# A transformer block with window attention: FC1 and the query/key projection regrouped into 128 + 64 channels

## The chip, the cores and the metric

The kernel runs on one core of a Trainium2 chip. The metric is the time of one execution on the device, in microseconds. TensorE (PE in the profile) multiplies, with the loads of its stationary operand shown apart (PEld); VectorE (DVE), ScalarE (ACT) and GpSimd (POOL) work on elements; SyncE (SP) issues every transfer of this kernel.

## What is computed

Inputs are 32 images of 96 channels and 56 x 56 pixels, in float32. The block is a Swin block with windows of 7 x 7 pixels (49 tokens), shifted by 3 pixels, and 12 heads of 8 channels:

```python
f = roll(layernorm(x over channels) * g1 + b1, (-3, -3))        # windows of 49 tokens
q, k, v = split(win @ w_qkv + b_qkv)                            # 96 -> 3 x 96
attn = softmax(q @ k.T * 8**-0.5 + mask); out = (attn @ v) @ w_proj + b_proj
f = x + unroll(out)
m = layernorm(f over channels) * g2 + b2
result = f + gelu(m @ w_fc1 + b_fc1) @ w_fc2 + b_fc2            # 96 -> 192 -> 96
```

## The kernel before

A **band** is one row of 8 windows, 7 x 56 pixels or 392 tokens (`TOK`); there are 8 bands in an image and 256 in all. The engines run the same software pipeline, written out by hand: at step t each engine works on several bands, each at another stage (`LOAD` t+9, `TURN` t+6, `BACK` t+5, `QK` t+4, `KEYS` t+3, scores t+2, probabilities t, and so on). Steps alternate between an odd and an even kind with another order. Two steps are one round of the pattern, and there are 128 such pairs. Engines are ordered by semaphores alone, and each engine runs its instructions in the written order.

The stages that matter here:

- `turn` transposes a band to tokens (L472), `back` transposes the normalised tokens back to channels (L487). `back_high` and `back_low` split the result in two float16 parts, `xfh` and `xfl`, whose row 96 of ones carries the bias.
- `queries_keys` (every step) and `expand` (twice in an odd step, FC1 of two bands) multiply by a weight of 192 output channels. They do it in two halves of 96 channels, each by `three` (L379): three products over all 392 tokens (high x high, high x low, low x high) into one PSUM bank of 96 partitions. So each use is 6 matmuls, 96 columns of weights by 392 tokens.
- In an odd step both uses of `expand` stand between `turn` and `max_transpose` (L511); then come `out_transposes` (L522), `back` (L487), `queries_keys` and `project` (L532). `back` waits for `gelu_done` of both FC1 results, since ScalarE has to empty the banks. In an even step `queries_keys` stands between `max_transpose` and `project`, and `contract` (FC2 of two bands, L559, float32) follows.
- ScalarE's `gelu` (L660) reads 96 x 784 of PSUM, `queries_keys_high` (L638) reads as many and writes the high parts to `nat`; VectorE's `queries_keys_low` (L772) writes the low parts.
- `values` (L395), `scores` (L414), `shifted` (L430) and `weighted` (L446) use 49 columns of weights, alternately for PSUM partitions 0 to 48 and 64 to 112.
- SP stores `nat` to a DRAM page per band with two transfers (`save_parts`, L286 and L289), and loads it again, reordered: `key_blocks` into `qst` and `kbd` (5 transfers, L258 and L260), `stacks` into `kst` and `qbd` (5 transfers). Before `key_blocks` SP waits until the high parts have landed in the page (`high_out`). `scores` waits for `key_in`, the five landings of `key_blocks`.
- FC2's bias is a row of `w2` against a row of ones in `hid`.
- VectorE's `result` adds `f` to FC2's output, two or more steps after `turn` has read that `f`.

Of the kernel before, what the change touches and what calls it, by code (L numbers as in the profile page):

```python
# [55 lines left out]
GAIN = 64.0  # L56
# [36 lines left out]
def build(nc, x, g1, b1, wqkv, bqkv, wproj, bproj, g2, b2, wfc1, bfc1, wfc2, bfc2,  # L93
# [7 lines left out]
    with ctx:  # L101
        def sb(name, shape, dt=F32):
            return ctx.enter_context(nc.sbuf_tensor(name, shape, dt))
# [12 lines left out]
        wp, w2 = sb("wp", [FULL, C]), sb("w2", [FULL, 2, C])  # L116
        vec = sb("vec", [C, 5])
        G1, B1, BP, G2, B2 = range(5)
# [7 lines left out]
        nat = sb("nat", [C, 4, 4, TOK], F16)  # L126
# [12 lines left out]
        hid = sb("hid", [FULL, 2, 2, TOK])  # L139
# [6 lines left out]
        stack_pages = nc.dram_tensor("stack_pages", [4, 2 * (side + 3 * TOK)], F16, kind="Internal").ap()  # L146
        q_stack = [stack_pages[n, 0:side].rearrange("(c m t) -> c m t", m=3, t=TOK) for n in range(4)]
        k_stack = [stack_pages[n, TOK + side:TOK + 2 * side].rearrange("(c m t) -> c m t", m=3, t=TOK) for n in range(4)]
        both_parts = [stack_pages[n, TOK:TOK + 2 * side].rearrange("(s c m t) -> c s m t", s=2, m=3, t=TOK)[:, :, 0:2, :] for n in range(4)]
        high_parts = [stack_pages[n].rearrange("(s r) -> s r", s=2)[:, 0:side].rearrange("s (c m t) -> c s m t", m=3, t=TOK)[:, :, 0, :] for n in range(4)]  # L150
# [12 lines left out]
        STACK_IN, KEY_IN = 5 * 16, 5 * 16  # L163
        X_IN = [16] * 7 + [2 * 16]
# [10 lines left out]
        ot_made, o_in, proj_made, f_made = sem("ot_made"), sem("o_in"), sem("proj_made"), sem("f_made")  # L175
        fc1_made, gelu_done, fc2_made, y_made = sem("fc1_made"), sem("gelu_done"), sem("fc2_made"), sem("y_made")
# [39 lines left out]

        @block.sync
        def _(sp):
# [10 lines left out]
            const(wp[0:C, :], wproj)  # L229
            for m in range(2):  # L230
                const(w2[0:C, m, :], wfc2[m * C:(m + 1) * C, :])
            const(w2[C:C + 1, 0, :], bfc2.rearrange("(a c) -> a c", a=1))
            const(brow[C:C + 1, :], bqkv.rearrange("(a c) -> a c", a=1))
            const(brow1[C:C + 1, :], bfc1.rearrange("(a c) -> a c", a=1))
            for n, v in ((G1, g1), (B1, b1), (BP, bproj), (G2, g2), (B2, b2)):
                column(n, v)
# [15 lines left out]
            def key_blocks(b):  # L252
# [3 lines left out]
                sp.wait_ge(high_out[b.c % 4], b.used(4, 16))  # L256
# [6 lines left out]
            def stacks(b):  # L263
# [3 lines left out]
                sp.wait_ge(nat_out[n], b.used(4, 16))  # L267
# [12 lines left out]
            def save_parts(b):  # L280
# [33 lines left out]
        def _(pool):  # L314
# [21 lines left out]

            def normalise(b):
# [19 lines left out]
            def step(t):  # L357
                if turns(t.step(TURN)):
                    normalise(t.step(TURN))
                if has(t.step(ORDER)):  # L360
                    order_x(t.step(ORDER))

# [3 lines left out]
        def _(pe):  # L366
# [123 lines left out]
            def queries_keys(t):  # L490
# [9 lines left out]
                for m in range(2):  # L500
                    last = three(psum[0:C, at + m, 0:TOK], wh[:, m * C:(m + 1) * C], wl[:, m * C:(m + 1) * C], b, 0)
                last.then_inc(qk_made, 1)
# [31 lines left out]
            def expand(t, n):  # L534
# [9 lines left out]
                for m in range(2):  # L544
# [322 lines left out]
```

## Time and profile before

| | |
|---|---|
| median of 3 runs | 3063.34 us (3062.35 to 3064.25) |
| the profiled execution, whole | 3062.91 us |
| its span, first to last instruction | 3061.1 us |
| mean granted clock of TensorE | 0.992 of full speed |
| TensorE matmul busy | 2862.6 us (94%) |
| VectorE, ScalarE, GpSimd busy | 2424.3, 2076.6, 1454.5 us (79%, 68%, 48%) |
| mean busy share of the DMA queue of SP | 43.7% of 16 engines |

Busy times are unions over the engine's instructions. A matmul's recorded length is from its start to the end of its results, and matmuls overlap, so the distance from start to start is what one costs in a row of them. In the trace, "128x392" is the moving operand and "128\*96" the stationary one; a float32 matmul that is no transpose appears as two passes. "[0.47 <-issue]" behind a row is the idle time before it and what ended it.

### The profile page before, as it was taken

What the parts mean: (1) busy time and instruction counts of PE and PEld (TensorE: products, weight loads), DVE (VectorE), ACT (ScalarE), POOL (GpSimd) and SP (SyncE); (2) the same over time, 40 slices, a digit from 0 to 9 for tenths busy, and PEclk for the clock granted to TensorE, in tenths of its full rate; (3) what the DMA queues carried; (4) which work ended last, traced back from release to release, by engine and by line L of the source; (5) the groups of instructions that cost most, each with busy time, mean ns of one, the idle gap of its engine ahead of it and who ended that gap; (6) DMA issues with size and microseconds to landing.
All of it is one profiled execution on the core that took longest, in us unless ns stands there. A gap on an engine that the chain in (4) does not pass through costs nothing.

```text
span 3061.1 us, 137479 instructions
## 1 busy us (share of the span) xinstructions
PE 2862.6 (94%) x53060; PEld 2299.2 (75%) x53060; DVE 2424.3 (79%) x7208; ACT 2076.6 (68%) x3208; POOL 1454.5 (48%) x1832
## 2 busy tenths in 40 slices
PE   1799999999999999999999999999999999999997
PEld 0677777777777777777777777777777777777775
DVE  5778888788887888788787888878888788888885
ACT  0467767667776767767766767767767667777674
POOL 2554454454444444444444454444454454445444
PEclk9899999999999999999999999999999999999999
DMA  1444444444444444444444444444444444444441
GB/s 29 108 119 123 124 125 119 119 126 122 126 127 113 123 123 122 126 121 120 124 126 114 125 124 120 124 123 120 123 125 118 120 126 121 126 127 119 125 113 42
DMA packets 414727, 359.37 MB, mean 117 GB/s; under 512 B 63455, under 2 KB 413985, under 8 KB 414012
## 3 DMA queue, kind: packets, MB, share of 16 engines
q1 hardware_dynamic: 414028, 350.01, 43.7%
q8 instruction: 444, 7.27, 1.1%
q14 instruction: 255, 2.09, 0.2%
HBM read 193.25 MB, written 154.14 MB: 113 GB/s over the span
## 4 chain that ended last, share of the span: by engine, by line
PE 87%; issue 5%; ACT 5%; DVE 2%; POOL 1%; SPq 0%; DMA 0%; POOLq 0%; DVEq 0%; ACTq 0%
PE psum L446 18%; PE psum L379 16%; PE psum L559 11%; PE psum L430 10%; PE psum L414 8%; PE psum L472 7%; PE psum L487 6%; PE psum L532 5%; ACT probs L618 4%; PE psum L522 3%; PE psum L395 2%; PE psum L511 1%; DVE st L754 1%; POOL rs L349 0%; DVE xfl L765 0%
## 5 line engine op out<-in xcount | busy, mean ns | idle before, releaser
L618 ACT ACTIVATE probs<-psum 113x784 f32<-113x784 f32 x768 | 633.2, 824 | 652.0 <-PE psum L430 648.9
L730 DVE TENSOR_REDUCE nmax<-psum 113x16 f32<-113x784 f32 x768 | 745.3, 970 | 153.9 <-PE psum L414 153.3
L342 POOL TENSOR_SCALAR ve<-mv 98x8 f32<-98x8 f32 x264 | 64.5, 244 | 1482.4 <-DVE mv L759 1476.5
L446 PE MATMUL psum<-vbd,probs 128*49 128x18 f32 x24576 | 644.2, 198 | 9.8 <-issue 9.0
L446 PEld LDWEIGHTS psum<-vbd,probs 128*49 128x49 f32 x24576 | 634.4, 126 | 14.1 <-issue 13.3
L349 POOL TENSOR_TENSOR rs<-ve,half 98x8 f32<-98x8 f32 x264 | 440.0, 1667 | 0.0
L430 PE MATMUL psum<-qbd,kst 128*49 128x196 f16 x6144 | 405.1, 251 | 36.3 <-DVE xfl L765 23.2
L754 DVE BATCH_NORM_STATS2 st<-tok 98x6 f32<-98x96 f32 x2112 | 363.6, 245 | 84.3 <-ACT tok L625 70.8
L354 POOL TENSOR_TENSOR xn<-xn,rs 98x768 f32<-98x768 f32 x264 | 388.4, 1471 | 72.7 <-POOL rs L349 72.7
L414 PE MATMUL psum<-kbd,qst 128*49 128x196 f16 x6144 | 401.4, 250 | 7.6 <-issue 4.2
L765 DVE TENSOR_TENSOR xfl<-psum,xfh 96x784 f16<-96x784 f32 x264 | 256.0, 970 | 176.0 <-ACT xfh L630 174.2
L345 POOL TENSOR_TENSOR xn<-tok,mv 98x768 f32<-98x768 f32 x264 | 389.5, 1475 | 0.2 <-POOL ve L342 0.2
L559 PE MATMUL psum<-hid,w 128*96 128x392 f32 x1024 | 359.3, 494 | 0.9 <-ACT hid L660 0.9
L430 PEld LDWEIGHTS psum<-qbd,kst 128*49 128x49 f16 x6144 | 238.8, 104 | 142.1 <-issue 103.0
L414 PEld LDWEIGHTS psum<-kbd,qst 128*49 128x49 f16 x6144 | 265.0, 104 | 85.3 <-issue 80.6
L559 PEld LDWEIGHTS psum<-hid,w 128*96 128x96 f32 x1024 | 167.4, 164 | 171.9 <-issue 170.6
L638 ACT ACTIVATE nat<-psum 96x784 f16<-96x784 f32 x256 | 209.9, 820 | 121.0 <-PE psum L379 121.0
L487 PE MATMUL psum<-ident,xn 98*96 98x98 f32 x2112 | 227.8, 252 | 64.9 <-issue 57.1
L630 ACT ACTIVATE xfh<-psum 96x784 f16<-96x784 f32 x264 | 215.3, 815 | 78.3 <-PE psum L487 78.2
L612 ACT ACTIVATE vbd<-psum 49x384 f32<-49x384 f32 x512 | 261.1, 510 | 7.6 <-PE psum L395 1.1
L487 PEld LDWEIGHTS psum<-ident,xn 98*96 98x96 f32 x2112 | 189.3, 128 | 91.0 <-issue 81.1
L772 DVE SCALAR_TENSOR_TENSOR nat<-psum,nat 96x784 f16<-96x784 f32 x256 | 245.7, 960 | 0.0
(83 smaller groups left out, 5270.1 us busy)
## 6 DMA issues: line engine op xcount, KB each, us to landing
stack_pages<-nat SPq DMA_DIRECT2D x256, 294.0 KB, 3.0
kst<-stack_pages SPq DMA_DIRECT2D x256, 220.5 KB
qbd<-stack_pages SPq DMA_DIRECT2D x1024, 55.1 KB
stack_pages<-nat SPq DMA_DIRECT2D x256, 147.0 KB, 2.0
xr<-in_x_dram SPq DMA_DIRECT2D x224, 147.0 KB, 3.4
out_dram<-yr SPq DMA_DIRECT2D x224, 147.0 KB, 2.2
qst<-stack_pages SPq DMA_DIRECT2D x256, 73.5 KB
kbd<-stack_pages SPq DMA_DIRECT2D x1024, 18.4 KB
```

The source lines that it names most:

```text
L345: nc.gpsimd.tensor_tensor(xn[:, n, :, :], tok[:, n, :, :, :].rearrange("t k p c -> t (k p) c"), mv[:, n, :, 0:1].to_broadcast(wide_by_toke ...
L349: nc.gpsimd.tensor_tensor(rs[:, n, :], ve[:, n, :], half[0:PT, :], ALU.pow).then_inc(root_done, 1)
L354: nc.gpsimd.tensor_tensor(xn[:, n, :, :], xn[:, n, :, :], rs[:, n, :].rearrange("t (g a) -> t g a", a=1).to_broadcast(wide_by_token), ALU. ...
L379: last = nc.tensor.matmul(dst, weights, tokens[:, b.c % 4, kind, :], start=n == 0, stop=n == 2)
L414: last = nc.tensor.matmul(psum[W1 * w:W1 * w + L, A + p // 2, p % 2 * CH:(p % 2 + 1) * CH], qst[:, masked_slot(b), u, toks], kbd[:, b.c % ...
L430: last = nc.tensor.matmul(psum[W1 * w:W1 * w + L, B + p // 2, p % 2 * CH:(p % 2 + 1) * CH], kst[:, masked_slot(b), u, toks], qbd[:, b.c % ...
L446: last = nc.tensor.matmul(dst[:, :, h, :], probs[:, b.c % 2, h // 4, p, h % 4 * L:(h % 4 + 1) * L], vbd[:, b.c % 4, p * NH + h, :, :], sta ...
L487: last = nc.tensor.transpose(psum[0:C, B + kind, p * PT:(p + 1) * PT], xn[:, b.c % 2, kind * PAIRS + p, :], ident[0:PT, 0:PT])
L559: last = nc.tensor.matmul(psum[0:C, D + n, 0:TOK], w2[:, m, :], hid[:, b.c % 2, m, :], start=m == 0, stop=m == 1)
L618: nc.scalar.activation(probs[0:PR, b.c % 2, u, :, :].rearrange("j (g q) k -> j g (q k)", g=2), psum[0:PR, B:B + 2, 0:2 * CH], ACT.Exp).the ...
L730: nc.vector.tensor_reduce(dst, psum[0:PR, A:A + 2, 0:2 * CH].rearrange("i g (q h j) -> i g q h j", q=2, j=L), axis=AX.X, op=ALU.max, negat ...
L754: last = nc.vector.bn_stats(st[:, n, g, :], tok[:, n, g // PAIRS, g % PAIRS, :])
```

## The change

FC1 and the queries and keys now make the first 128 of their 192 output channels for all 392 tokens (3 matmuls with 128 columns of weights), and the other 64 channels for each half of the tokens apart (`PART`, 196): 6 matmuls with 64 columns, alternately for PSUM partitions 0 to 63 and 64 to 127. The result stands as 128 x 3 x 196 in PSUM where it was 96 x 2 x 392. ScalarE's GELU and high parts and VectorE's low parts read that in one instruction each. FC2 has `w2` in three parts and makes each half of the tokens with two matmuls. Row 97 of `hid` and `w2` is no longer there for the bias, so GpSimd adds FC2's bias to `f` in place, in a new stage `add_bias`, and `result` waits for it. `save_parts` needs 4 transfers for the high parts and 3 for both parts, 7 where there were 2.

```diff
+PART = TOK // 2
+REST = HID - 128
+BIAS = -4
-        wp, w2 = sb("wp", [FULL, C]), sb("w2", [FULL, 2, C])
+        wp, w2 = sb("wp", [FULL, C]), sb("w2", [FULL, 3, C])
-        nat = sb("nat", [C, 4, 4, TOK], F16)
+        nat = sb("nat", [FULL, 4, 2, 3, PART], F16)
-        hid = sb("hid", [FULL, 2, 2, TOK])
+        hid = sb("hid", [FULL, 2, 3, PART])
+        def three_parts(bank):
+            return psum[:, bank:bank + 2, :].rearrange("p b (s r) -> p (b s) r", s=2)[:, 0:3, 0:PART]
...
-                sp.dma_start(high_parts[n], nat[:, n, 0:4:2, :]).then_inc(high_out[n], 16)
+                most = nat[:, n, 0, 0:2, :].rearrange("c s t -> c (s t)")
+                sp.dma_start(pages[n][0:C, 0, :], most[0:C]).then_inc(high_out[n], 16)
+                sp.dma_start(pages[n][C + 1:FULL + 1, 0, :], most[C:FULL]).then_inc(high_out[n], 16)
+                for s in range(2):
+                    sp.dma_start(pages[n][FULL + 1:2 * C + 1, 0, s * PART:(s + 1) * PART], nat[REST * s:REST * (s + 1), n, 0, 2, :]).then_inc(high_out[n], 16)
...
-                sp.dma_start(both_parts[n], nat[:, n, :, :].rearrange("c (s m) t -> c s m t", s=2)).then_inc(nat_out[n], 16)
+                sp.dma_start(pages[n][0:FULL, 1:3, :], nat[:, n, :, 0:2, :].rearrange("c m s t -> c m (s t)")).then_inc(nat_out[n], 16)
+                for s in range(2):
+                    sp.dma_start(pages[n][FULL:2 * C, 1:3, s * PART:(s + 1) * PART], nat[REST * s:REST * (s + 1), n, :, 2, :]).then_inc(nat_out[n], 16)
...
+            def add_bias(b):
+                pool.wait_ge(t_made, b.step(AFTER).count(1, 1))
+                alone(pool)
+                nc.gpsimd.tensor_scalar(f[:, b.c % 8, :], f[:, b.c % 8, :], vec[:, BF:BF + 1], None, ALU.add).then_inc(f_biased, 1)
...
-            def three(dst, high, low, b, kind):
-                for n, (weights, tokens) in enumerate(((high, xfh), (high, xfl), (low, xfh))):
-                    last = nc.tensor.matmul(dst, weights, tokens[:, b.c % 4, kind, :], start=n == 0, stop=n == 2)
+            def most_and_rest(bank, high, low, b, kind):
+                products = ((high, xfh), (high, xfl), (low, xfh))
+                for n, (weights, tokens) in enumerate(products):
+                    nc.tensor.matmul(three_parts(bank)[:, 0:2, :], weights[:, 0:FULL], tokens[:, b.c % 4, kind, :].rearrange("c (s t) -> c s t", s=2),
+                                     start=n == 0, stop=n == 2)
+                for n, (weights, tokens) in enumerate(products):
+                    for s in range(2):
+                        last = nc.tensor.matmul(psum[REST * s:REST * (s + 1), bank + 1, 0:PART], weights[:, FULL:FULL + REST], tokens[:, b.c % 4, kind, s * PART:(s + 1) * PART],
+                                                start=n == 0, stop=n == 2)
                 return last
...
-                for m in range(2):
-                    last = nc.tensor.matmul(psum[0:C, D + n, 0:TOK], w2[:, m, :], hid[:, b.c % 2, m, :], start=m == 0, stop=m == 1)
+                for s in range(2):
+                    dst = psum[0:C, D + n, s * PART:(s + 1) * PART]
+                    nc.tensor.matmul(dst, w2[:, 0, :], hid[:, b.c % 2, s, :], start=True, stop=False)
+                    last = nc.tensor.matmul(dst, w2[:, 1 + s, :], hid[:, b.c % 2, 2, :], start=False, stop=True)
...
-                nc.scalar.activation(nat[0:C, b.c % 4, 0:4:2, :], psum[0:C, at:at + 2, 0:TOK], ACT.Copy, scale=1 / GAIN).then_inc(qk_high, 1)
+                nc.scalar.activation(nat[:, b.c % 4, 0, :, :], three_parts(at), ACT.Copy, scale=1 / GAIN).then_inc(qk_high, 1)
-                nc.scalar.activation(hid[0:C, b.c % 2, :, :], psum[0:C, at:at + 2, 0:TOK], ACT.Gelu, scale=1 / GAIN).then_inc(gelu_done, 1)
+                nc.scalar.activation(hid[:, b.c % 2, :, :], three_parts(at), ACT.Gelu, scale=1 / GAIN).then_inc(gelu_done, 1)
...
+                dve.wait_ge(f_biased, b.count(1, 1))
```

`add_bias` is the last stage of a step on GpSimd, for band t-4, whose `f` was read by `turn` at TensorE's step t-2.

## Rows read from the trace of the kernel before

**Rows 1.** The page: busy time by engine, and the chain that ended last by engine.

```profile
PE 2862.6 (94%) x53060; PEld 2299.2 (75%) x53060; DVE 2424.3 (79%) x7208; ACT 2076.6 (68%) x3208; POOL 1454.5 (48%) x1832
...
PE 87%; issue 5%; ACT 5%; DVE 2%; POOL 1%; SPq 0%; DMA 0%; POOLq 0%; DVEq 0%; ACTq 0%
```

**Rows 2.** Matrix engine by time, even step: start, length, line, operands, count.

```profile
1502.53 0.51 PE L414 MATMUL psum<-kbd,qst 128*49 128x196 f16 x8
1502.97 0.54 PE L472 MATMUL psum<-ident,xw 96*98 96x96 f32 x4
1503.34 0.49 PE L472 MATMUL psum<-ident,f 96*98 96x96 f32 x4
...
1504.84 0.33 PE L379 MATMUL psum<-xfh,wh 128*96 128x392 f16 x1
...
1505.83 0.82 PE L532 MATMUL psum<-oT,wp 128*96 128x392 f32 x2
1506.49 2.80 PE L559 MATMUL psum<-hid,w 128*96 128x392 f32 x8
1509.22 0.53 PE L430 MATMUL psum<-qbd,kst 128*49 128x196 f16 x8
...
1510.09 0.51 PE L414 MATMUL psum<-kbd,qst 128*49 128x196 f16 x8
1510.44 0.32 PE L446 MATMUL psum<-vbd,probs 128*49 128x18 f32 x8
```

**Rows 3.** Matrix engine by time, odd step.

```profile
1515.03 0.34 PE L379 MATMUL psum<-xfh,w1h 128*96 128x392 f16 x1
...
1516.87 0.33 PE L379 MATMUL psum<-xfh,w1l 128*96 128x392 f16 x1
1517.03 0.26 PE L511 MATMUL psum<-ident,nmax 113*48 113x113 f32 x1
...
1518.15 0.85 PE L487 MATMUL psum<-ident,xn 98*96 98x98 f32 x8 [0.47 <-issue]
```

**Rows 4.** Instruction groups by shape: busy us, mean ns of one, idle before.

```profile
L652 ACT ACTIVATE oT<-psum 96x196 f32<-96x196 f32 x512 | 139.3, 325 | 3.8 <-PE psum L522 3.8
...
L331 POOL COPY xw<-xr 96x343 f32<-96x343 f32 x256 | 126.5, 494 | 36.0 <-DMA xr<-in_x_dram 36.0
...
L532 PEld LDWEIGHTS psum<-oT,wp 128*96 128x96 f32 x512 | 82.7, 163 | 12.8 <-ACT oT L652 0.8
...
L342 POOL TENSOR_SCALAR ve<-mv 98x8 f32<-98x8 f32 x264 | 64.5, 244 | 1482.4 <-DVE mv L759 1476.5 <-PE psum L487 5.9
...
L379 PEld LDWEIGHTS psum<-xfh,w1h 128*96 128x96 f16 x512 | 62.5, 122 | 22.0 <-issue 1.6
```

**Rows 5.** ScalarE by time, odd step.

```profile
1514.91 1.28 ACT L660 ACT_TABLE_LOAD   x1
1516.24 0.82 ACT L660 ACTIVATE hid<-psum 96x784 f32<-96x784 f32 x1
1517.23 0.82 ACT L660 ACTIVATE hid<-psum 96x784 f32<-96x784 f32 x1 [0.17 <-PE psum L379]
```

**Rows 6.** Waits of the matrix engine, whole span: total us, times, longest.

```profile
PE psum L487 <- issue: 57.1, 120, 1.0
```

**Rows 7.** Transfers issued by SP, by time: start, length of the issues.

```profile
1502.99 1.36 SPq L260 DMA_DIRECT2D kbd<-stack_pages  x4
...
1507.39 0.44 SPq L286 DMA_DIRECT2D stack_pages<-nat  x1
1509.55 0.31 SPq L289 DMA_DIRECT2D stack_pages<-nat  x1
1510.18 1.48 SPq L250 DMA_DIRECT2D xr<-in_x_dram  x1
```

**Rows 8.** Waits of SP, whole span: total us, times, longest.

```profile
SPq L204 <- DVE nat L772: 473.9, 254, 5.4
```

**Rows 9.** The page: transfers by kind, KB of one, median us to landing.

```profile
stack_pages<-nat SPq DMA_DIRECT2D x256, 294.0 KB, 3.0
```

More of the change, by code:

```diff
@@ L115, in build @@
         w1h, w1l = sb("w1h", [FULL, HID], F16), sb("w1l", [FULL, HID], F16)
-        wp, w2 = sb("wp", [FULL, C]), sb("w2", [FULL, 2, C])
-        vec = sb("vec", [C, 5])
-        G1, B1, BP, G2, B2 = range(5)
+        wp, w2 = sb("wp", [FULL, C]), sb("w2", [FULL, 3, C])
+        vec = sb("vec", [C, 6])
+        G1, B1, BP, G2, B2, BF = range(6)
         xr = sb("xr", [C, 4, WS, SIDE])
@@ L145, in build @@
         side = C * 3 * TOK
[L146 to L150, printed above, removed]
+        stack_pages = nc.dram_tensor("stack_pages", [4, 2 * side + 3 * TOK], F16, kind="Internal").ap()
+        pages = [stack_pages[n].rearrange("(c m t) -> c m t", m=3, t=TOK) for n in range(4)]
+        q_stack, k_stack = ([stack_pages[n, at:at + side].rearrange("(c m t) -> c m t", m=3, t=TOK) for n in range(4)] for at in (0, TOK + side))
         consts_in, filled, rows_one, vbd_zero, vbd_ones = sem("consts_in"), sem("filled"), sem("rows_one"), sem("vbd_zero"), sem("vbd_ones")
@@ L163, in build @@
         STACK_IN, KEY_IN = 5 * 16, 5 * 16
+        HIGH_OUT, NAT_OUT = 4 * 16, 3 * 16
         X_IN = [16] * 7 + [2 * 16]
@@ L229, in _ @@
             const(wp[0:C, :], wproj)
+            const(w2[:, 0, :], wfc2[0:FULL, :])
             for m in range(2):
-                const(w2[0:C, m, :], wfc2[m * C:(m + 1) * C, :])
-            const(w2[C:C + 1, 0, :], bfc2.rearrange("(a c) -> a c", a=1))
+                const(w2[REST * m:REST * (m + 1), 1 + m, :], wfc2[FULL:HID, :])
             const(brow[C:C + 1, :], bqkv.rearrange("(a c) -> a c", a=1))
             const(brow1[C:C + 1, :], bfc1.rearrange("(a c) -> a c", a=1))
-            for n, v in ((G1, g1), (B1, b1), (BP, bproj), (G2, g2), (B2, b2)):
+            for n, v in ((G1, g1), (B1, b1), (BP, bproj), (G2, g2), (B2, b2), (BF, bfc2)):
                 column(n, v)
@@ L361, in step @@
                     order_x(t.step(ORDER))
+                if has(t.step(BIAS)):
+                    add_bias(t.step(BIAS))
             steps(pool, step)
@@ L499, in queries_keys @@
                     pe.wait_ge(s_maxed, t.step(SCORE).count(QUADS, QUADS))
-                for m in range(2):
-                    last = three(psum[0:C, at + m, 0:TOK], wh[:, m * C:(m + 1) * C], wl[:, m * C:(m + 1) * C], b, 0)
-                last.then_inc(qk_made, 1)
+                most_and_rest(at, wh, wl, b, 0).then_inc(qk_made, 1)
             def max_transpose(t):
@@ L543, in expand @@
                     pe.wait_ge(s_maxed, t.step(SCORE).count(QUADS, QUADS))
-                for m in range(2):
-                    last = three(psum[0:C, (B, A)[n] + m, 0:TOK], w1h[:, m * C:(m + 1) * C], w1l[:, m * C:(m + 1) * C], b, 1)
+                last = most_and_rest((B, A)[n], w1h, w1l, b, 1)
                 last.then_inc(fc1_made, 1)
@@ L635, in queries_keys_high @@
                 act.wait_ge(qk_made, b.count(1, 1))
-                wait(act, nat_out[b.c % 4], b.step(-4).used(4, 16))
-                wait(act, high_out[b.c % 4], b.step(-4).used(4, 16))
-                nc.scalar.activation(nat[0:C, b.c % 4, 0:4:2, :], psum[0:C, at:at + 2, 0:TOK], ACT.Copy, scale=1 / GAIN).then_inc(qk_high, 1)
+                wait(act, nat_out[b.c % 4], b.step(-4).used(4, NAT_OUT))
+                wait(act, high_out[b.c % 4], b.step(-4).used(4, HIGH_OUT))
+                nc.scalar.activation(nat[:, b.c % 4, 0, :, :], three_parts(at), ACT.Copy, scale=1 / GAIN).then_inc(qk_high, 1)
             def max_rows(t):
@@ L697, in _ @@
                 nc.vector.memset(a[:, :, :, :], 0.0)
-            for a in (wide, wide1, wp, w2, xfh, xfl, oT, hid, kst, probs):
+            nc.vector.memset(w2[:, 1:3, :], 0.0)
+            for a in (wide, wide1, wp, xfh, xfl, oT, kst, probs):
                 last = nc.vector.memset(a[FILL:FULL], 0.0)
@@ L770, in queries_keys_low @@
                 dve.wait_ge(qk_high, b.count(1, 1))
-                parts = nat[0:C, b.c % 4, :, :]
-                nc.vector.scalar_tensor_tensor(out=parts[:, 1:4:2, :], in0=psum[0:C, at:at + 2, 0:TOK], scalar=1 / GAIN, in1=parts[:, 0:4:2, :],
+                parts = nat[:, b.c % 4, :, :, :]
+                nc.vector.scalar_tensor_tensor(out=parts[:, 1], in0=three_parts(at), scalar=1 / GAIN, in1=parts[:, 0],
                                                op0=ALU.mult, op1=ALU.subtract).then_inc(qk_low, 1)
```

11 lines of the change are left out of this document (5 added, 6 removed).

## The prediction

> **What bounds the kernel now.** I read the page first. The matrix engine is busy 94% of the span and holds 87% of the chain that ended last; ScalarE and time put down to "issue" hold 5% each, and no transfer is in it [rows 1]. So what counts is how long TensorE's row of instructions is, and where it waits. Next comes the engine by time. The pattern repeats in pairs of steps, 128 times; one pair takes about 23.3 us (L414 opens an even step, L430 the odd one), at full clock. Two things are to be seen there. In the even step nothing around the changed lines waits: L379, L532, L559 and L430 follow each other without an idle time [rows 2]. In the odd step there is one real hole, 0.47 us ahead of `back` (L487) [rows 3]. It occurs 120 times and sums to 57.1 us [rows 6]. ScalarE's rows say what it is: the second GELU starts 0.04 us after the last FC1 product ends, runs 0.82 us to 1518.05, and L487 starts 0.10 us later [rows 5, 3]. So in the odd step the path is FC1, second GELU, `back`; everywhere else it is the matrix engine alone.
>
> **Prices, read from rows.** A product of 392 tokens: six in 0.99 us, eleven in 1.84 us, so 0.166 us each [rows 2, 3]. Alternating column halves: eight matmuls of 196 tokens take 0.35 us from 1510.09 to 1510.44, four pairs, so 0.087 us a pair; one alone streams 196 tokens in about 0.083, so both halves of a pair run side by side [rows 2].
>
> Going over from full width to halves: L559's eight passes at 0.33 (two L532 passes in 0.66) should give 2.64 us to L430, and there are 2.73: 0.09 more. The first group behind such an edge is also longer, 0.53 against 0.51: the load of 49 columns, otherwise hidden, shows with 0.02. I take 0.03 for 64 columns, so 0.12 for an edge inwards [rows 2].
>
> From halves to full: L414 at 1502.53 to L472 at 1502.97 is 0.44 where a group takes 0.35: 0.09 more. The first four transposes last 0.54, the next four 0.49: a load of 98 columns shows with 0.05 [rows 2]. For 128 columns I take 0.065, for the 48 of L511 0.02. L532's float32 load takes 163 ns where L379's takes 122 for as many columns [rows 4], so 0.08. Edges outwards cost 0.15 (second FC1), 0.11 (L511) and 0.17 (L532). That the loads lie open I infer from these small differences; with them hidden an edge is a bare 0.09, the lower bound. The upper bound is twice the load read. The nearest rows, of the same kind of instruction, say the values taken.
>
> **The change part by part, per pair of steps.**
>
> *The products.* Each use goes from 6 x 0.166 = 0.996 to 3 x 0.166 + 3 x 0.087 = 0.759, 0.237 less, four times in a pair. But each use brings two edges, eight in all. The two FC1 uses: 2 x 0.759 + 0.12 + 0.15 + 0.12 + 0.11 = 2.02 us where there are 2.00 [rows 3]. Nothing is won. Each use for queries and keys: 0.759 + 0.12 + 0.17 = 1.05 where there are 0.99 [rows 2]: 0.06 lost, 0.12 for the two.
>
> *The second GELU.* It reads 588 columns in place of 784. From L652 (196 columns, 325 ns) and L660 (784, 0.82 us), ScalarE pays 0.84 ns a column, so 0.655 us, 0.165 less [rows 4, 5]. It also starts sooner: the last pair of FC1 starts at 1515.03 + 1.518 + 0.39 - 0.087 = 1516.85 and ends 0.25 later (0.51 less three spacings [rows 2]) at 1517.10, against 1516.87 + 0.33 = 1517.20 now [rows 3]. The first GELU is not in its way: it starts when its table has been loaded, 1516.24, and would end at 1516.90 [rows 5]. So `back` starts 0.265 us sooner, and the hole shrinks from 0.47 to about 0.18 (L511 and L522 come 0.02 later). This is the gain of the whole change.
>
> *FC2.* Sixteen passes of 196 tokens for eight of 392. The streaming is the same; splitting costs between nothing and 8 x 0.009 (two pair spacings are 0.175, one product 0.166). I take 0.02. Their loads of 0.16 us length stay under the passes, as the loads of L472 do, one every 0.08 us [rows 2].
>
> *VectorE and ScalarE elsewhere.* `queries_keys_low` and `queries_keys_high` get a quarter shorter too, some 0.2 and 0.165 us. I cost this at nothing: the even step's next consumer, L430, does not wait for them now [rows 2]. The bias wait of `result` is met two steps ahead.
>
> *GpSimd.* `add_bias` works on 96 x 392. A copy of 343 columns takes 494 ns [rows 4], so 0.5 to 0.8 us. It stands last in the step, ahead of the wait for statistics before L342, which is 1482 / 264 = 5.6 us a step [rows 4]; that covers it. Without this cover it would delay `normalise` by as much.
>
> *Seven transfers.* Five more issues a band at 0.34 us (four of `kbd` in 1.36 [rows 7]) are 1.7 us of SP's time. SP waits 1.85 us a band for VectorE's low parts alone [rows 8], and for other things besides. What is queued behind: three more high transfers stand ahead of the wait for the low parts (L286 at 1507.39, L289 at 1509.55 [rows 7]), where 1.0 us fits into 1.7. Two more low ones stand ahead of `load_x`, `key_blocks`, `stacks` and `maxima`, which all go 0.7 us later. The first of them that an engine needs are the keys: issued until 1504.35 [rows 7], wanted by L414 at 1510.09 [rows 2]; with the 3.0 us that a page transfer takes to land [rows 9], 2.7 us are left, 2.0 after the change. Cost: nothing, and up to some tenths a pair if stalls like L250's issue of 1.48 us [rows 7] come together. At the start one constant more is loaded, 0.3 us, once.
>
> **Sum.** -0.265 + 0.12 + 0.02 = -0.125 us a pair, times 128 = -16 us. The profiled execution took 3062.9 us, 0.4 below the median, with 1.8 around its span; I subtract from the median: 3047 us.
>
> **The rivals.**
>
> 1. *Loads at the edges hidden, bare edges.* Then 0.125 goes before the second GELU and each use for queries and keys is 0.759 + 0.18 = 0.94: -0.39 - 0.10 + 0.02 = -0.47 a pair, 3003 us. Against it speak the 0.53 and the 0.54 [rows 2].
>
> 2. *The halves cost what they promise, no edges.* FC1's second GELU would then be bound by the first, 1516.24 + 0.655 + 0.04 + 0.655 = 1517.59, 0.46 sooner; queries and keys 2 x 0.237 less: -0.46 - 0.47 + 0.02 = -0.91, 2947 us. The 0.09 at both kinds of edge speaks plainly against it [rows 2]. The Trainium skill, TensorEngine Tiling (Array Packing), Theoretical Speedup, promises up to twice the speed for 64 columns or fewer; for the pairs in a row the trace bears that out, at the edges it does not.
>
> 3. *No difference.* Edges 0.02 dearer than read, which is about how well hundredths can be read: seven edges lie on the path (three before the second GELU, four around queries and keys), 0.14 a pair, so +0.015, 3065 us. The Trainium skill, TensorE: Matmul & The Clock Gate, LDWEIGHTS, gives a load as its columns divided by 1.2 per ns; by it 64 columns lie open for 0.053 and 128 for 0.107, and the sum would come to this rival's. The trace's 0.02 for 49 and 0.05 for 98 are half of that rule.
>
> 4. *The keys come late (slower).* SP's 1.7 us more and the small transfers push `key_blocks` past `scores`. It decides from 2.0 us of further delay on; a late landing of 0.5 us a pair gives +0.375, 3111 us, and 0.17 is enough to be slower than before. For it: SP has some stalls over 1 us [rows 7]. Against: the waits it has left [rows 8].
>
> 5. *The pairs don't overlap* with 64 columns: 0.237 more a use, +0.82 a pair, 3168 us. L414's pairs with 49 columns speak against it [rows 2].
>
> 6. *Edges dearer still*, 0.03 to 0.05 each: 3074 to 3092 us. No row of before goes from a float16 product of full clock straight into halves.
>
> **How the numbers follow.** Forecast 0.41; rivals in their order 0.10, 0.03, 0.22, 0.10, 0.04, 0.10. About 0.2% (6 us) is what a measurement of this kernel can tell from no change. Faster: the forecast less its upper end (0.39) and rivals 1 and 2, 0.52. Same: rival 3 and that end, 0.24. Slower: rivals 4 to 6, 0.24. The range reaches from rival 1 to the dear edges, 3000 to 3092 us; it leaves out rivals 2 and 5 and the worse part of 4, about 0.13. The forecast's own range is 3037 to 3057.
>
> **What would show it.** FC1 from first product to L511 near 2.02 us, L379's successor from first product to L532 near 1.05; the first pair of a group of halves 0.12 behind the last full product's stream; GELU at 0.655 us; the wait ahead of L487 near 0.18. Scores never waiting for keys. Wrong would make me: an edge other than 0.11 to 0.17, since eight of them stand against a saving of as much, or an idle time ahead of L414.

## The result, and the profile after

The changed kernel takes 3227.15 us (median of 4 runs, 3223.39 to 3236.5), against 3062.85 us for the kernel before, run beside it (3059.53 to 3064.25): a ratio of 1.0543, with a 95% interval of 1.0519 to 1.0567. The forecast was 3047 us. The time is above the top of the range too, 3092.

The page names the new bound. Busy time by engine, the DMA totals, and the chain that ended last by engine and by line:

```profile
PE 2932.0 (91%) x55620; PEld 2368.2 (73%) x55620; DVE 2372.9 (74%) x7206; ACT 1999.3 (62%) x3208; POOL 1773.5 (55%) x2088
...
DMA packets 533727, 359.83 MB, mean 112 GB/s; under 512 B 182429, under 2 KB 532959, under 8 KB 532986
q1 hardware_dynamic: 533002, 350.11, 42.6%
...
SPq 72%; issue 15%; PE 8%; DVE 2%; POOL 1%; ACT 1%; DMA 1%; DVEq 0%; POOLq 0%; ACTq 0%
SPq L277 12%; SPq L301 10%; SPq L266 9%; SPq L296 9%; SPq L293 5%; SPq L284 5%; SPq L294 4%; SPq L256 4%; SPq L299 4%; SPq L307 3%; SPq L264 3%; SPq L275 2%; PE psum L472 2%; SPq L207 1%; PE psum L456 1%
```

The busy line alone would mislead: the matrix engine still reads 91%. Its share of the chain fell from 87% [rows 1] to 8%, and SPq, which stood at 0%, holds 72%. SPq is SP's instruction queue, and the lines are its `dma_start` calls. L293 to L301 are the seven page transfers that stand where two stood; L256, L264 to L284 and L307 are old ones. The DMA queue itself is at 42.6%, against 43.7% before: it isn't the queue that has filled up, but the row of starts.

Waits of SP and of the matrix engine, changed kernel: total us, times, longest:

```profile
SPq L207 <- DVE yr L820: 51.1, 10, 15.4
SPq L207 <- ACT nat L663: 25.3, 9, 14.4
...
SPq L207 <- DVE nat L797: 3.9, 8, 1.5
```

```profile
PEld psum L440 <- DMA kbd<-stack_pages: 194.6, 139, 3.1
```

In the kernel before SP waited 473.9 us for VectorE's low parts [rows 8]; now it waits 3.9. SP is hardly ever early any more. And the matrix engine's load for the scores (L440, before L414) waits 139 times for the keys, 194.6 us in all.

SP's issues by time, one band from L293 to the next L293: start, length of the issues, line, names, count:

```profile
1508.62 0.32 SPq L293 DMA_DIRECT2D stack_pages<-nat  x1
1508.99 0.42 SPq L294 DMA_DIRECT2D stack_pages<-nat  x1
1509.45 1.13 SPq L296 DMA_DIRECT2D stack_pages<-nat  x2
1510.99 0.77 SPq L299 DMA_DIRECT2D stack_pages<-nat  x1
1511.80 1.27 SPq L301 DMA_DIRECT2D stack_pages<-nat  x2
1513.41 0.33 SPq L256 DMA_DIRECT2D xr<-in_x_dram  x1
1513.99 0.32 SPq L264 DMA_DIRECT2D qst<-stack_pages  x1
1514.37 1.34 SPq L266 DMA_DIRECT2D kbd<-stack_pages  x4
1515.90 0.31 SPq L275 DMA_DIRECT2D kst<-stack_pages  x1
1516.25 2.97 SPq L277 DMA_DIRECT2D qbd<-stack_pages  x4
1519.34 0.58 SPq L284 DMA_DIRECT2D qbd<-mrow  x1
1520.18 0.36 SPq L293 DMA_DIRECT2D stack_pages<-nat  x1
```

The issues down to L284 sum to 9.76 us of the 11.56 that the band takes. The other 1.80 us are eleven gaps, 0.04 to 0.12 between most lines and 0.19 to 0.41 in front of five of them; nowhere is there a gap like the 1.72 us ahead of L289 [rows 7]. Seven page transfers here take 0.32 + 0.42 + 1.13 + 0.77 + 1.27 = 3.91 us.

Over the whole run, the groups of the page transfers: ns min/median/max, first and last start, forms:

```profile
L293 SPq DMA_DIRECT2D stack_pages<-nat x256: 318/439/1927, 68.9 to 3151.6; - x128
L294 SPq DMA_DIRECT2D stack_pages<-nat x256: 404/418/1809, 69.3 to 3152.0; - x128
L296 SPq DMA_DIRECT2D stack_pages<-nat x512: 484/596/2044, 69.8 to 3154.0; - x171
L301 SPq DMA_DIRECT2D stack_pages<-nat x512: 597/616/2057, 71.7 to 3155.9; - x171
```

The medians are 418 to 616 ns, and single issues take up to 2 us. In the mean the seven come to 4.48 us a band, the two of before to 0.70. Added up from the trace's records between 300 and 2700 us, per pair of steps: SP's issue time goes from 12.38 to 19.58 us, its gaps between issues grow by some 0.45, and its idle time falls from 6.74 to 0.42. So 7.65 us were added and 6.32 of them found idle time; 1.33 are left over, and the pair grows from 22.94 to 24.37 us, by 1.43. That carries the loss: the growth is 0.87 and 0.75 us a pair in the first and last 32 bands and 1.2 to 1.7 between, together the 164 us.

### The profile page after: what moved, and what is told of

Its sections match the earlier page's. It is cut to its first block, busy times and chain, and to the rows that moved or that the text cites. A ratio compares the mean times of both kernels' runs of the same rounds, so it can differ in the third digit from the quotient of the medians.

```text
span 3225.1 us, 144483 instructions
## 1 busy us (share of the span) xinstructions
PE 2932.0 (91%) x55620; PEld 2368.2 (73%) x55620; DVE 2372.9 (74%) x7206; ACT 1999.3 (62%) x3208; POOL 1773.5 (55%) x2088
## 2 busy tenths in 40 slices
DMA packets 533727, 359.83 MB, mean 112 GB/s; under 512 B 182429, under 2 KB 532959, under 8 KB 532986
## 3 DMA queue, kind: packets, MB, share of 16 engines
q1 hardware_dynamic: 533002, 350.11, 42.6%
## 4 chain that ended last, share of the span: by engine, by line
SPq 72%; issue 15%; PE 8%; DVE 2%; POOL 1%; ACT 1%; DMA 1%; DVEq 0%; POOLq 0%; ACTq 0%
SPq L277 12%; SPq L301 10%; SPq L266 9%; SPq L296 9%; SPq L293 5%; SPq L284 5%; SPq L294 4%; SPq L256 4%; SPq L299 4%; SPq L307 3%; SPq L264 3%; SPq L275 2%; PE psum L472 2%; SPq L207 1%; PE psum L456 1%
## 5 line engine op out<-in xcount | busy, mean ns | idle before, releaser
L472 PE MATMUL psum<-vbd,probs 128*49 128x18 f32 x24576 | 660.8, 200 | 8.8 <-issue 8.5
L472 PEld LDWEIGHTS psum<-vbd,probs 128*49 128x49 f32 x24576 | 651.4, 129 | 12.4 <-issue 11.8
L440 PE MATMUL psum<-kbd,qst 128*49 128x196 f16 x6144 | 411.9, 255 | 138.1 <-DMA kbd<-stack_pages 125.3
L456 PE MATMUL psum<-qbd,kst 128*49 128x196 f16 x6144 | 413.2, 256 | 34.0 <-DVE xfl L790 23.3
L440 PEld LDWEIGHTS psum<-kbd,qst 128*49 128x49 f16 x6144 | 271.6, 106 | 228.8 <-DMA kbd<-stack_pages 194.6
L353 POOL TENSOR_SCALAR f<-f,vec 96x392 f32<-96x392 f32 x256 | 324.3, 1267 | 0.0
L456 PEld LDWEIGHTS psum<-qbd,kst 128*49 128x49 f16 x6144 | 246.6, 106 | 95.6 <-issue 59.7
L513 PE MATMUL psum<-ident,xn 98*96 98x98 f32 x2112 | 228.3, 252 | 31.9 <-issue 25.4
L583 PE MATMUL psum<-hid,w 128*96 128x196 f32 x1024 | 254.2, 330 | 0.8 <-ACT hid L685 0.8
L584 PE MATMUL psum<-hid,w 128*96 128x196 f32 x1024 | 253.8, 329 | 0.0
L513 PEld LDWEIGHTS psum<-ident,xn 98*96 98x96 f32 x2112 | 189.7, 128 | 58.1 <-issue 49.6
L556 PE MATMUL psum<-oT,wp 128*96 128x392 f32 x512 | 229.9, 531 | 0.4 <-ACT mrow L669 0.4
```

The source lines that it names most:

```text
L353: nc.gpsimd.tensor_scalar(f[:, b.c % 8, :], f[:, b.c % 8, :], vec[:, BF:BF + 1], None, ALU.add).then_inc(f_biased, 1)
L440: last = nc.tensor.matmul(psum[W1 * w:W1 * w + L, A + p // 2, p % 2 * CH:(p % 2 + 1) * CH], qst[:, masked_slot(b), u, toks], kbd[:, b.c % ...
L456: last = nc.tensor.matmul(psum[W1 * w:W1 * w + L, B + p // 2, p % 2 * CH:(p % 2 + 1) * CH], kst[:, masked_slot(b), u, toks], qbd[:, b.c % ...
L472: last = nc.tensor.matmul(dst[:, :, h, :], probs[:, b.c % 2, h // 4, p, h % 4 * L:(h % 4 + 1) * L], vbd[:, b.c % 4, p * NH + h, :, :], sta ...
L513: last = nc.tensor.transpose(psum[0:C, B + kind, p * PT:(p + 1) * PT], xn[:, b.c % 2, kind * PAIRS + p, :], ident[0:PT, 0:PT])
```

## What TensorE's own row shows

Even step of the changed kernel, matrix engine by time, as in [rows 2] and [rows 3]:

```profile
1515.47 0.26 PE L535 MATMUL psum<-ident,nmax 113*48 113x113 f32 x1
1515.57 0.33 PE L400 MATMUL psum<-xfh,wh 128*128 128x392 f16 x1
...
1515.91 0.33 PE L400 MATMUL psum<-xfh,wl 128*128 128x392 f16 x1
1516.16 0.28 PE L404 MATMUL psum<-xfh,wh 128*64 128x196 f16 x2
1516.27 0.25 PE L404 MATMUL psum<-xfl,wh 128*64 128x196 f16 x2
1516.36 0.25 PE L404 MATMUL psum<-xfh,wl 128*64 128x196 f16 x2
1516.54 0.90 PE L556 MATMUL psum<-oT,wp 128*96 128x392 f32 x2
```

From the last full product to the first pair of halves there are 0.25 us (0.258 in the median of 197) where 0.166 would do: an edge of 0.09. From the last pair to L556 there are 0.18 where a pair takes 0.09: 0.09 again. The first pair stays 0.11 long, 0.02 more than the next: the load of 64 columns. L556's pair of passes takes 0.90 where L532's took 0.82 [rows 2]: 0.08 for its load. The use takes 0.97 to L556's start and 1.05 with that load.

Odd step, the stretch ahead of `back`, and the GELU's group by shape (busy us, mean ns of one, idle before):

```profile
1504.59 0.33 PE L400 MATMUL psum<-xfh,w1l 128*128 128x392 f16 x1
1504.85 0.28 PE L404 MATMUL psum<-xfh,w1h 128*64 128x196 f16 x2
...
1505.05 0.25 PE L404 MATMUL psum<-xfh,w1l 128*64 128x196 f16 x2
1505.23 0.28 PE L535 MATMUL psum<-ident,nmax 113*48 113x113 f32 x1
1505.34 0.55 PE L546 MATMUL psum<-ident,on 113*96 113x113 f32 x4
1506.10 0.85 PE L513 MATMUL psum<-ident,xn 98*96 98x98 f32 x8 [0.21 <-issue]
```

```profile
L685 ACT ACTIVATE hid<-psum 128x588 f32<-128x588 f32 x256 | 169.1, 660 | 51.2 <-PE psum L404 49.9
L353 POOL TENSOR_SCALAR f<-f,vec 96x392 f32<-96x392 f32 x256 | 324.3, 1267 | 0.0
```

The GELU takes 660 ns, and the hole ahead of `back` (L513, before L487) is 0.21 where it was 0.47 [rows 3]. On this engine the change does nearly what the prediction reads. `add_bias` takes 1267 ns, 1.6 times the upper end of 0.8.

One thing is left out of these rows. The first FC1 use of this same step, from 1502.35 on, ran with 0.33 us from product to product, at the lower of TensorE's two clock levels (1.2 GHz; granted clock 0.50 from 1494.5 to 1504.3), which followed a long wait for the keys:

```profile
1493.93 0.64 PE L440 MATMUL psum<-kbd,qst 128*49 128x196 f16 x8 [2.28 <-DMA kbd<-stack_pages]
```

## Theories

**S, SP is the bound.** Seven transfers cost SP more than the forecast's 0.34 us each, and its row, with no slack left, sets the period. Rivals: **P**, the small packets: those under 512 B went from 63455 to 182429, so transfers land late, whoever issues them. **G**, GpSimd's long `add_bias` delays `normalise`. **E**, edges dearer than read; the rows above speak against it already. **C**, the clock: 0.975 granted in the mean where it was 0.992. **W**, next to these, is for the hole ahead of `back`: it is wholly the wait for the second GELU.

## Experiments on the slowdown

**FC1 alone.** FC1, FC2 and the bias as changed; queries and keys with `three`, and two transfers as before (the diff is against the changed kernel and shows the first lines).

```diff
-                most_and_rest(at, wh, wl, b, 0).then_inc(qk_made, 1)
+                for m in range(2):
+                    last = three(psum[0:C, at + m, 0:TOK], wh[:, m * C:(m + 1) * C], ...)
```

> Only FC1, FC2 and the bias on GpSimd are changed as in the changed kernel; queries and keys and their two page transfers are as before. Theory S (SP, which issues every transfer one after the other, has become the bound, by 7 issues where there were 2): SP has no more to do than before, so what is left is the gain on the odd step's path, 0.24 us a pair of steps: 3030 to 3040 us, ratio 0.990 to 0.993. Theory E (edges between full width and column halves on TensorE are dearer than forecast): three edges lie ahead of the second GELU here, so it would be no faster than before, 3065 to 3100 us. Theory G (the bias on GpSimd, 1.27 us where 0.5 to 0.8 was forecast, delays the normalised tokens): over 3065 us, with waits for GpSimd's xn.

Measured: 3031.33 us, ratio 0.9897 (0.9878 to 0.9916), the hole 0.20 us, and SP waits again for the low parts, 497.3 us in 256 times. `add_bias` is in it, so G falls; E falls too, by which this kernel would be no faster than before. The gain is 30 us, 0.24 us for each of 128 pairs; the forecast's terms for this part, -0.265 and +0.02, give 0.245. FC1 by its first product, and the first row behind its last one:

```profile
1504.73 0.33 PE L402 MATMUL psum<-xfh,w1h 128*128 128x392 f16 x1
...
1506.67 0.28 PE L539 MATMUL psum<-ident,nmax 113*48 113x113 f32 x1
```

That is 1.94 us (also the median of 105 steps), where there were 2.00.

**Seven transfers alone.** The kernel before, the same bytes in seven transfers.

```diff
-                sp.dma_start(high_parts[n], nat[:, n, 0:4:2, :])...
+                keys = high_parts[n][:, 1, :]
+                sp.dma_start(high_parts[n][:, 0, :], nat[:, n, 0, :])...
+                sp.dma_start(keys[0:32], nat[0:32, n, 2, :])...
+                for s in range(2):
+                    sp.dma_start(keys[32:C, s * 196:(s + 1) * 196], nat[32:C, n, 2, s * 196:...])...
```

and `both_parts` in three in the same way.

> The kernel before with the same bytes sent to the pages by 7 transfers in place of 2 (4 of high parts, 3 of both parts), and nothing else changed on any engine. Theory S: slow like the changed kernel, 3190 to 3250 us, ratio 1.04 to 1.06, with SP's waits for other engines gone. Theory P (not the issues, but the smaller packets fill the DMA rings and the keys land late): slow too, but the more packets under 512 B, the slower; it has as many of them as the changed kernel or more. Theory E or G: 3063 us, since no engine that computes does anything else.

Measured: 3142.61 us, 1.0261 (1.0234 to 1.0288). SPq holds 66% of the chain, and SP issues 18.88 us a pair in a period of 23.59. The direction is S's, the size was overrated: SP's issues take 0.70 us a pair less than in the changed kernel, 0.44 of it in the seven page transfers (4.26 us a band for 4.48). It also speaks against P: this kernel has 215007 packets under 512 B, more than the changed one, and loses half as much.

**Queries and keys alone.** The complement of the first: `most_and_rest` and seven transfers for queries and keys, FC1, GELU, FC2 and bias as before.

> Only queries and keys are regrouped, with the 7 transfers; FC1, FC2 and the bias are as before. Theory S: within 0.5% of the changed kernel, 3210 to 3240 us, as SP has the same to do. Theory G: back near the time before, 3063 to 3085 us, since GpSimd's bias is gone. Theory E: half of the loss at most, since four of eight edges are gone, 3110 to 3150 us.

Measured: 3201.4 us, 1.0467 (1.0439 to 1.0494), a little under the expected range; SPq holds 73% of the chain, SP issues 19.36 us a pair, period 24.07. The loss belongs to this half of the change.

**The same transfers, but SP relieved.** The changed kernel; `load_x` and `store_y` move to GpSimd. Packets under 512 B remain 182429.

```diff
-                    sp.dma_start(xr[:, b.c % 4, at:at + rows, :], ...)
+                    nc.gpsimd.dma_start(xr[:, b.c % 4, at:at + rows, :], ...)
-                    sp.dma_start(out[b.image(), :, row:row + rows, :], ...)
+                    nc.gpsimd.dma_start(out[b.image(), :, row:row + rows, :], ...)
```

> The changed kernel with the loads of x and the stores of the result issued by GpSimd instead of SP; the same bytes, packets and page transfers. Theory S: SP gets rid of two issues a band with their waits and address arithmetic (1.0 to 1.2 us of 12.6), so TensorE is the bound again, or nearly: 3040 to 3090 us, ratio 0.993 to 1.009. Theory P: the rings carry the same packets, so it stays slow, 3190 to 3250 us. Theory G: slower than the changed kernel, over 3230 us, since GpSimd gets still more to do.

Measured: 3035.73 us, 0.9909 (0.9886 to 0.9932). Its chain that ended last, by engine:

```profile
PE 86%; ACT 4%; issue 4%; DVE 2%; SPq 1%; POOL 1%; DMA 0%; DVEq 0%; POOLq 0%; ACTq 0%
```

The matrix engine is back, and its wait for `kbd` falls to 4.8 us in 6 times. Same bytes, same small packets, another issuer of x and y. By itself this leaves a doubt, since x and y now also go through another queue (q0, software_dynamic, at 8.6%; SP's is at 35.7%, it was at 42.6%). But seven transfers alone had more small packets and lost less, so P is refuted and S stands. C falls as well: the granted clock is 0.987 here and with FC1 alone, which both gain 1%, and 0.988 with seven transfers alone, which lose 2.6%. Of the changed kernel's own loss the clock can hold no more than SP's remaining idle time, 0.42 us a pair, unless it lengthened SP's issues, which no run separates. This kernel is also the change without its SP bound: 3036 us where the forecast says 3047.

**Small transfers for their number alone.** The kernel before with 5, then 10, more transfers a band from SP, each of 16 rows of 392 bytes to a scratch page that nobody reads (the wait is for those of four bands before).

```diff
+                wait(sp, small_out[n], b.step(-4).used(4, 16 * 5))
+                alone(sp)
+                for j in range(5):
+                    sp.dma_start(scratch[n, j], ident[0:16, 0:98]).then_inc(small_out[n], 16)
```

> The kernel before with 5 more transfers a band on SP behind the low parts, of 16 x 392 bytes from a constant to an unused page: 10 more issues a pair of steps, as many as the change adds, but with 6 KB each and of a cheap shape. Theory S (SP's time in issues decides): 10 x 0.35 to 0.45 = 3.5 to 4.5 us in a pair where SP idles 6.7, so hidden: 3060 to 3090 us, ratio 1.000 to 1.010. Theory N (the number of transfers decides): as slow as seven page transfers, 3140 us or more.

> The same with 10 more a band, 20 a pair: 7 to 9 us more of SP's time than before, over its 6.7 us of idle time. Theory S: SP has become the bound, by 0.3 to 2.3 us a pair: 3110 to 3360 us, and SP's waits for the computing engines are gone. Theory P (bytes and packets in the rings decide): 60 KB more a band, an eighth of the traffic, rings at half their capacity: no more than 3080 us.

Measured: 3089.03 us, 1.0106 (1.0087 to 1.0126), and 3629.98 us, 1.1883 (1.1852 to 1.1913). Ten more: the chain and the matrix engine's wait.

```profile
SPq 71%; issue 14%; PE 10%; DVE 3%; DMA 2%; ACT 1%; POOL 0%; POOLq 0%; DVEq 0%; ACTq 0%
```

```profile
PEld psum L420 <- DMA kbd<-stack_pages: 428.5, 200, 5.7
```

The second lay far above what I expected, 3110 to 3360. It settles P once more: 145375 packets under 512 B, fewer than in the changed kernel, and more than three times its loss. (The ten add 4.6% to the bytes, 366 MB for 350, and not the eighth that I had expected.) Its granted clock fell to 0.929, with TensorE waiting 200 times for the keys; how much of the 3630 us is the clock's is not shown. SP's issue time a pair against the period, both in us from the trace's records, orders six kernels:

```
before              12.38   22.94
five small more     17.94   23.09
seven transfers     18.88   23.59
queries/keys alone  19.36   24.07
changed kernel      19.58   24.37
ten small more      22.13   27.53
```

The period rises by 0.15 us for the first 5.56 us of issues, by 0.50 for the next 0.94 (five small to seven), by 0.78 for the next 0.70, and at the end by 3.16 for 2.55, where the gaps of ten more issues, at 0.043 us each, bring the 2.55 to 2.98. A slack is used up, and from there every microsecond of SP counts whole.

**The price of one issue.** The kernel before, with series of six transfers at its end, each shape first with its landing awaited, then back to back; its total time means nothing.

```diff
+            def rows96x784(i): return scratch[i, 0:96, 0, :], nat[0:96, 0, 0, :]
...
+            for i in range(6):
+                sp.dma_start(*rows96x784(i)).then_inc(probe, 16)
+                sent += 16
+                sp.wait_ge(probe, sent)
+            for i in range(6):
+                sp.dma_start(*rows96x784(i)).then_inc(probe, 16)
+                sent += 16
+            sp.wait_ge(probe, sent)
```

> The kernel before, and behind its last store a series of transfers from SBUF to an unused DRAM page, shape by shape: six that each wait for the one before to land, then six back to back. Theory S1 (an issue costs by its shape, whatever goes before): the shapes of the changed kernel cost 0.42 us (96 x 784 bytes), 0.42 (32 rows), 0.60 (64 x 392), 0.61 (64 x 2 x 392) in both kinds of series, and 96 x 2 x 784 costs 0.31. Theory S2 (an issue costs 0.3 us alone and the rest is waiting for the descriptors of the one before): about 0.3 us for all when each has landed, and 0.4 to 0.6 only back to back. The whole is some 150 to 250 us longer than before, which says nothing else.

Groups by line: ns min/median/max. L336 and L340 are 96 rows of 784 bytes (awaited, back to back), L344 and L348 64 rows of 784, L404 transfers of 96 x 2 pieces of 784, back to back.

```profile
L336 SPq DMA_DIRECT2D scratch<-nat x6: 303/303/310, 3063.9 to 3071.9; - x6
L340 SPq DMA_DIRECT2D scratch<-nat x6: 304/426/428, 3073.5 to 3075.7; - x6
L344 SPq DMA_DIRECT2D scratch<-nat x6: 445/446/512, 3077.5 to 3086.9; - x6
L348 SPq DMA_DIRECT2D scratch<-nat x6: 445/596/597, 3088.8 to 3091.9; - x6
L404 SPq DMA_DIRECT2D scratch<-nat x6: 305/472/480, 3184.9 to 3187.3; - x6
```

An issue costs 303 ns if the one before has landed, 426 back to back, and 0.14 to 0.17 more with 64 rows: 446 and 596. 16, 32, 48 and 128 rows cost what 96 do, within 20 ns, and 392 bytes what 784 do. Neither S1 nor S2 holds alone: shape and spacing both count. Why 64 rows are dear stays open. L296's 596 above is just such, and L301's 616 is 64 x 2 pieces of 392 bytes, 607 in this probe: the two halves of a rest are 64 rows each, sent back to back.

## Experiments on the gain

**The hole alone.** The kernel before; `back` waits for the first GELU in place of the second. `back` writes bank B, which the first GELU reads; the second reads A, and `contract` waits for both itself. So the reason given ahead for the wait, that ScalarE has to empty the banks, holds for the first GELU only.

```diff
-wait(pe, gelu_done, t.step(HIDDEN[1]).count(1, 1)) if has(t.step(HIDDEN[1])) else None
+wait(pe, gelu_done, t.step(HIDDEN[0]).count(1, 1)) if has(t.step(HIDDEN[0])) else None
```

> The kernel before, in which `back` waits for the first GELU of the odd step only (that of the bank that it overwrites), no longer for the second. Theory W (the whole gain of the regrouped FC1 comes from this wait, since the GELU is shorter): the hole of 0.47 us idle, 0.64 us beyond the usual spacing, goes: 2985 to 3005 us, ratio 0.975 to 0.981. Rival X (the gain comes from TensorE's cheaper products, the wait is only where it shows): the wait comes back elsewhere in the step, over 3040 us.

Measured: 2981.25 us, 0.9744 (0.9723 to 0.9766), a little better than expected. From L522 to L487 there are 1.02 us before (1517.13 to 1518.15 [rows 3]), and then this kernel:

```profile
1517.13 0.55 PE L522 MATMUL psum<-ident,on 113*96 113x113 f32 x4
```

```profile
1503.60 0.55 PE L522 MATMUL psum<-ident,on 113*96 113x113 f32 x4
1503.98 0.84 PE L487 MATMUL psum<-ident,xn 98*96 98x98 f32 x8
```

That is 0.38. So the hole cost 0.64 us, not the 0.47 that the wait shows [rows 3]: L522's row is 0.55 us long in both, and without the wait its last 0.17 lie under L487. 0.64 in 120 pairs are 77 us, and 3059.3 - 2981.25 = 78.

**FC1 regrouped, without the hole.** The first experiment with this wait.

> The FC1-only kernel with the same one wait changed. Theory W: without the wait, a regrouped FC1 with its four edges is worth nothing: within 0.5% of the previous kernel (before, with the wait changed), 2985 to 3010 us. Rival X: the products are cheaper by themselves, so it is 25 to 60 us faster than that kernel, 2930 to 2965 us.

Measured: 2988.24 us, 0.9769 (0.975 to 0.9787). So W: without the hole the regrouped FC1 wins nothing, it is 7 us behind the kernel before with the same edit (the slowest of four runs there took 2984.54 us, the fastest here 2987.14). The prediction's working has nothing won either, 2.02 us for 2.00, and 0.02 for FC2. By the records it isn't that simple: FC1 is 0.06 us shorter, its next row 0.02 and FC2 0.02 longer, so 0.02 a pair should be left; where these and the 7 us go is not shown.

**Two edges fewer.** Both rests side by side: `expand(t)` makes the 128 channels (`most`) of the first use, both rests, and the 128 channels of the second (its body is left out here).

```diff
-                    expand(t, 0)
-                    expand(t, 1)
+                    expand(t)
```

> The FC1-only kernel, with the two FC1 uses in the order first 128 channels, first rest, second rest, second 128 channels, so that the two rests stand side by side: two edges in place of four, and L511 follows a full-width product. The wait for the second GELU is as it was. By the edges as read, the second GELU starts 0.10 to 0.12 us sooner: 13 to 15 us less than FC1 only, 3015 to 3020 us. If edges cost nothing there: 3031 us as FC1 only.

> The same order with `back` waiting for the first GELU only. Now the matrix engine alone is the bound in the odd step, and two edges less and the cheaper products count in full, 0.26 us a pair of steps: 30 to 35 us less than before with the wait changed, 2950 to 2970 us, ratio about 0.967. If ScalarE takes over as the bound of the odd step (two GELUs, outputs, maxima, high parts in a row): 2980 us or more.

Measured: 3018.87 us, 0.9869 (0.9848 to 0.9889), as expected, and with the early wait 2978.37 us, 0.9736 (0.9717 to 0.9755), where I expected 2950 to 2970. The edges are worth 9 to 12 us in the total. In the records they are worth more: FC1 takes 1.72 us in both kernels where it took 1.94, 0.11 for each edge with its load. What is missing in the second is at `turn` of the even step: its first transpose starts 0.30 us (median) after the last scores started, instead of 0.18, which is 16 us in 128 pairs. It starts 0.145 us behind the end of GpSimd's last copy in 94 of 108 steps, where it started 0.258 behind it with four edges. The list of waits shows little of this:

```profile
PE psum L500 <- POOL xw L343: 32.4, 18, 10.6
```

Of these, 30.0 us in 7 times are in the previous kernels too. So GpSimd came next, and I thought that it could be reordered.

**GpSimd reordered.** The last kernel, with `order_x` and `add_bias` ahead of `normalise`.

```diff
             def step(t):
-                if turns(t.step(TURN)):
-                    normalise(t.step(TURN))
                 if has(t.step(ORDER)):
                     order_x(t.step(ORDER))
                 if has(t.step(BIAS)):
                     add_bias(t.step(BIAS))
+                if turns(t.step(TURN)):
+                    normalise(t.step(TURN))
```

> The kernel with both FC1 rests together and `back` waiting for the first GELU, and on GpSimd the ordering of x and the bias now ahead of `normalise` in a step, not behind it. In the previous kernel TensorE's `turn` starts some 0.09 us behind the end of GpSimd's last copy, 0.12 us later than an edge alone would make it, so with the copies done in the idle time ahead of the statistics it gains 0.10 to 0.13 us a pair: 2960 to 2968 us. If something else sets `turn` back just as much: 2975 to 2980 us.

Measured: 3224.4 us, 1.0539 (1.0515 to 1.0562). The waits of this kernel:

```profile
POOL xw L339 <- DVE f L823: 1276.5, 248, 13.4
...
PE psum L515 <- POOL xn L368: 226.8, 127, 6.6
```

The even step's `turn` is back at 0.18 us, so the copies did hold it up. But I had counted only how long `order_x` takes, and not what it waits for. Its wait for `f`, 5.1 us each, now stands ahead of `normalise`, and the matrix engine waits for `xn` instead. It is the mistake of the prediction once more, on another engine.

The fastest kernel is FC1 with its rests together and the early wait, 2978 us; the kernel before with the early wait alone comes to 2981, and their intervals overlap. I would take the one-line edit.

## Why the prediction was wrong

*The step that failed is "Seven transfers", which ends with "Cost: nothing".* Two things in it were wrong. First the price: 0.34 us an issue was read from four `kbd` issues [rows 7]. The group as it stands in the change is 4.48 us for seven, so 3.8 us a band more and some 4.0 with the gaps between issues, where 1.7 were taken. This is a term sized less than half. Second the test that decided: the slack of the first consumer, the keys, 2.7 us of which 2.0 would be left. Slack to one consumer tells how late a transfer may be once. It doesn't tell whether SP's in-order row still fits into a pair. The prediction does set its 1.7 us against the 1.85 that SP waits a band for the low parts, and names "other things besides"; but it doesn't sum them, and so has no price at which the answer turns. SP's largest waits in the kernel before, beside the 473.9 us of [rows 8]:

```profile
SPq L204 <- ACT nat L638: 222.7, 166, 15.0
SPq L204 <- ACT mrow L644: 167.1, 115, 3.0
SPq L204 <- DVE yr L794: 54.9, 10, 15.7
```

Together they are 7.2 us a pair (6.7 of idle time by the records). With 3.4 (2 x 1.7) that fits, with 8 it doesn't. The second error made the first dangerous: with a slack of 7.2 us in view, ten more issues a pair have a price at which they decide, 0.72 us each, and L250's 1.48 us for one issue [rows 7] would have counted against "Cost: nothing". In its place the runs show SP's row as the bound: 19.58 us of issues in a period of 24.37, and a pair 1.43 us longer.

*A rival named what would be seen.* "The keys come late" is what happened: `key_blocks` late, L440 waiting for `kbd`. It had a chance of 0.10, and its 3111 us were too low, since the delay isn't a landing that is late by 0.5 us but a row of work 1.4 us longer than the pair. Its point of decision, 2.0 us of further delay, is passed: the seven take 4.0 us more a band, and SP's waits no longer take that up.

*The Trainium skill leans the same way.* DMA: Bandwidth & Descriptors, section "Issuing engines are not separate DMA queues", says that issuing from several engines saves only the sequencer's time to start a transfer, which is usually small beside the transfer. The trace agrees for one transfer: a page transfer's issue takes 0.42 to 0.62 us and its landing 1.9 to 2.4. But transfers overlap and SP's issues don't, and here their sum sets the period: the same transfers with x and y issued elsewhere, 3036 us for 3227.

*The edges were right, some of the loads too dear.* Read 0.09 and 0.02 inwards, found 0.09 and 0.02 (0.03 had been taken); outwards 0.09 plus the load, found 0.09 and 0.08 ahead of the projection. The use for queries and keys was forecast at 1.05 us and takes 1.05. FC1 was forecast at 2.02 and takes 1.94, 1.96 with the next load: the 0.065 for a load of 128 columns was an estimate, and the first product of the second use shows 0.01 to 0.02. Rivals 1 and 2 (no open loads, no edges), 5 (no overlap) and 6 (edges dearer still) are out, and so is rival 3's price of 0.02 more an edge.

*The gain was right.* GELU 0.655 forecast, 0.660 found; the hole 0.18 forecast, 0.20 and 0.21 found; the part for FC1 alone 0.245 us a pair forecast, 0.24 measured. Some of that is luck: by the medians of the records the path from FC1 to `back` is 0.31 shorter where 0.265 was forecast, for FC1 itself saves 0.04 with the row behind it. The halves gained next to nothing as matmuls, as the working says; the gain is a shorter GELU under a wait.

*`add_bias`* was sized at 0.5 to 0.8 us and takes 1.27. It is hidden as forecast, by GpSimd's wait for the statistics.

*The sum without SP* was 3047 us; 3036 measured, just below the forecast's own range. Of the 11 us between, the records give 8 to FC1 (0.06 us a pair) and 3 to queries and keys (0.10 a pair for 0.12). The totals would have it otherwise: the FC1 part alone took 3031, so queries and keys would cost 4 us and not 15. The intervals of the two runs overlap, so this stays open.

## What to carry to other kernels

When a change adds transfers, sum the issuing engine's whole row per period, issues and gaps, against all of its waits, and not only the slack to the first consumer; an engine without busy time in the page (SP here) can still be the bound, and only the chain and its own waits show it. Price an issue by rows of the same shape and spacing. Before reshaping work to shorten a stage that something waits for, ask whether the wait has to be there at all: one changed index was worth 78 us, while the regrouping of FC1 won 30 us beside the wait and nothing once it was gone. An engine that is kept waiting may then also run at a lower clock, so rows read right behind a wait need their granted clock beside them.

## What the hardware showed that I had not expected

An issue's time depends on its shape and on what is under way, not on its bytes: 303 ns awaited, 426 back to back, 446 and 596 with 64 rows, and single ones near 2 us in the full kernel. The same x load and y store, issued by GpSimd, cost that engine 592 and 516 ns in the mean (448 and 368 on SP in the changed kernel). A hole of 0.47 us in the matrix engine's records cost 0.64. Behind a wait of 2.28 us for the keys TensorE's granted clock was 0.50 for some 10 us. A `tensor_scalar` on GpSimd, 96 x 392 float32 in place, takes 1.27 us where a copy of 343 columns takes 0.49 [rows 4].
